# A decoder of six layers on one core: the small work of PEER, BiDAF and MoE placed differently

## The reference

```python
x = x + causal_attention(layernorm(x))
x = x + cross_attention(layernorm(x), ctx)
x = x + peer(layernorm(x))            # product-key experts
x = x + band_attention(layernorm(x))
x = x + bidaf(layernorm(x), ctx)
x = x + moe(layernorm(x))             # 8 experts, the top 2
```

## Time and profile before

| what | value |
|---|---|
| median of three runs | 3894.4 us |
| the profiled execution | 3891.91 us, its span 3889.9 us |
| busy, share of the span | PE 86%, DVE 71%, POOL 51%, ACT 30% |
| PEER | 913 to 2535 us |
| BiDAF | 2980 to 3262 us |
| MoE's head | 3262 to 3356 us |
| MoE's tiles | 3361 to 3890 us |

### The profile page before, as it was taken

The page is one execution under the profiler, slowest core; times in us unless marked ns, Lnnn a source line. Parts: engine busy times, 40 slices in busy tenths (PEclk is TensorE's granted clock), DMA queues, the critical chain, the costliest instruction groups (busy, mean ns, idle before and its releaser), DMA issues. The chain is left out here.

```text
span 3889.9 us, 93119 instructions
## 1 busy us (share of the span) xinstructions
PE 3336.4 (86%) x33694; PEld 2822.4 (73%) x33695; DVE 2759.0 (71%) x10928; ACT 1156.3 (30%) x2660; POOL 1993.4 (51%) x2200
## 2 busy tenths in 40 slices
PE   6999957875798998989999989878887888599998
PEld 4777735554688888888888888845564667599998
DVE  6666634556999999999999999768885443533333
ACT  1344435442222222222222222146663111122221
POOL 4444335540766666666666666768882000133332
PEclk8999969987899999999999999989997886699999
DMA  5444334442000000000000000045441002566665
GB/s 152 106 113 107 97 91 120 119 110 100 2 2 2 2 2 2 2 2 2 2 2 2 2 2 2 2 126 128 127 125 40 24 24 100 152 184 178 187 177 139
DMA packets 256102, 277.73 MB, mean 71 GB/s; under 512 B 44002, under 2 KB 200674, under 8 KB 255202
## 3 DMA queue, kind: packets, MB, share of 16 engines
q1 hardware_dynamic: 242081, 253.69, 22.8%
q0 software_dynamic: 13632, 18.91, 3.2%
HBM read 187.63 MB, written 72.29 MB: 67 GB/s over the span
## 5 line engine op out<-in xcount | busy, mean ns | idle before, releaser
L1163 POOL TENSOR_TENSOR peer_hot_v<-peer_hot_e,peer_parts 80x512 bf16<-80x512 bf16 x768 | 1045.0, 1386 | 456.4 <-DVE peer_hot_e L1202 443.2
L1008 PE MATMUL peer_ps_u<-peer_up,peer_g 128*128 128x256 f32 x2048 | 544.8, 414 | 0.6 <-DVE x_all L1319 0.6
L989 PEld LDWEIGHTS peer_ps_h<-peer_xnT,peer_down 128*128 128x128 f32 x4096 | 507.0, 195 | 17.0 <-DMA peer_down<-in_peer_down 2.5
L989 PE MATMUL peer_ps_h<-peer_xnT,peer_down 128*128 128x128 f32 x4096 | 506.9, 278 | 2.2 <-DMA peer_down<-in_peer_down 2.2
L999 PE MATMUL peer_ps_w<-peer_hot_v,peer_hot_u 80*128 80x32 bf16 x12288 | 347.7, 177 | 173.1 <-DVE peer_g L1214 111.7
L999 PEld LDWEIGHTS peer_ps_w<-peer_hot_v,peer_hot_u 80*128 80x128 bf16 x12288 | 336.5, 97 | 197.0 <-DVE peer_hot_u L1206 123.0
L1008 PEld LDWEIGHTS peer_ps_u<-peer_up,peer_g 128*128 128x128 f32 x2048 | 402.1, 206 | 56.7 <-issue 1.0
L1086 ACT ACTIVATE peer_g<-peer_ps_h 128x512 f32<-128x512 f32 x256 | 152.8, 597 | 904.8 <-PE peer_ps_h L989 904.7
L1206 DVE TENSOR_TENSOR peer_hot_u<-peer_count,peer_uvT 80x2048 bf16<-80x2048 bf16 x256 | 344.8, 1347 | 0.0
L2058 POOL DMA_INDIRECT moe_xg<-moe_xn_rows,moe_source x71 | 70.4, 991 | 420.7 <-DVE moe_target L2165 389.6
L2064 POOL DMA_INDIRECT out<-moe_y,moe_target x71 | 113.0, 1592 | 311.9 <-DVE moe_y L2195 308.9
(11 more groups left out here) (362 smaller groups left out, 6974.1 us busy)
## 6 DMA issues: line engine op xcount, KB each, us to landing
moe_w<-in_moe_w SPq DMA_DIRECT2D x142, 512.0 KB
causal_qs<-causal_qscratch SPq DMA_DIRECT2D x32, 384.0 KB, 3.9
cross_qs<-cross_qscratch SPq DMA_DIRECT2D x32, 384.0 KB, 3.7
band_qs<-band_qscratch SPq DMA_DIRECT2D x32, 384.0 KB, 4.0
moe_w<-in_moe_w SPq DMA_DIRECT2D x8, 1024.0 KB, 11.8
causal_qscratch<-causal_part SPq DMA_DIRECT2D x32, 192.0 KB, 2.6
causal_kscratch<-causal_part SPq DMA_DIRECT2D x32, 192.0 KB, 2.0
causal_ks<-causal_kscratch SPq DMA_DIRECT2D x32, 192.0 KB, 4.2
```

The source lines that it names most:

```text
L989: mm = nc.tensor.matmul(ps_h[:, n % 2, k * P:(k + 1) * P], down[:, c, 4 * n + k, :], xnT[:, par, c, :], start=(c == 0), stop=(c == DC - 1))
L1008: mm = nc.tensor.matmul(ps_u[:], g[:, par, v, :], up[:, v, :], start=(v == 0), stop=(v == EV - 1))
L1163: ins = nc.gpsimd.tensor_tensor(hot_v[0:SEL, n % RING, part], hot_e[0:SEL, n % RING], w, ALU.mult)
```

## The change

- PEER: `norm` and `candidates` go from DVE to POOL, at the start of `macro` ahead of the hots. The Exp becomes eight with `accum_out`, which also makes `es`, and the reduction on DVE goes.
- BiDAF: `halves` takes the place of `each`, fully written out. In each half-step h every part works on batch h minus its own lag. `project` is split in three; norm of c is on POOL. For MoE, each batch gets its own moments, roots (an integer guess and three Newton steps on DVE), normalised rows (POOL), store, transposes, logits and top choices, with lags of 2 to 4. The constants of MoE are made at half-step 3, and `w2` is loaded 1 MB at a time in half-steps 2 to 9. The tensors and semaphores for this are in a new `Route`, which is closed at the end of the kernel.
- MoE's head keeps what follows the top choices. One-hots are f16, in four groups of 8 tiles with 3 DVE instructions each; the name of a token is one f16 number, so 71 columns take the place of 142. `expert` is made after the first group, and SP's loads of w1 wait for it alone.

```diff
-                nc.scalar.activation(ew[:], ew[:], ACT.Exp).then_inc(exp_out, 1)
+                for h in range(NQ):
+                    ins = nc.scalar.activation(ew[:, h, :], ew[:, h, :], ACT.Exp, accum_out=es[:, h, :])
+                ins.then_inc(exp_out, 1)
...
+            def norm(t):
+                wait(pool, xt_done, t)
+                nc.gpsimd.tensor_scalar(xn[:], x_all[:, t, :], mean[:, t, :], rstd[:, t, :], ALU.subtract,
+                                        ALU.mult).then_inc(xn_ready, 1)
+
+            def candidates(t):
+                pool.wait_ge(halves_done, t + 1)
+                wait(pool, code_ready, t)
...
+                pool.wait_ge(roots_ready, 1)
+                norm(0)
+                norm(1)
+                candidates(0)
...
             def macro(t, par):
+                if there(t + 2):
+                    norm(t + 2)
+                if there(t + 1):
+                    candidates(t + 1)
...
-                steps.link(nc.vector.tensor_reduce(es[:], ew[:], AX.X, ALU.add))
...
+        def halves(steps):
+            for h in range(B + 5):
+                for part, back in steps:
+                    b = h - back
+                    if 0 <= b < B:
+                        part(streams[b % NS], b // NS, b)
...
+            for h in range(B + 4):
+                if h < B:
+                    fetch(streams[h % NS], h // NS, h)
+                if h == 1:
+                    weights()
+                if 0 <= h - 2 < B:
+                    store(streams[h % NS], (h - 2) // NS, h - 2)
+                if 0 <= h - 3 < B:
+                    store_rows(streams[(h - 3) % NS], (h - 3) // NS, h - 3)
+                if 2 <= h < 2 + E:
+                    sp.dma_start(route.w2[:, h - 2], w2_in[:, h - 2]).then_inc(route.weights, 16)
...
+                wait(pe, z.l_used, n - 1)
...
+            def project_a(z, n, b):
                 pe.wait_ge(z.a_used, n + 1)
+                for t in range(TT):
+                    tile = z.p3[:, t * D:(t + 1) * D]
+                    for c in range(DC):
+                        nc.tensor.matmul(tile, z.aT[:, c, t * P:(t + 1) * P], wl[:, DC + c, :], start=(t == 0 and c == 0), stop=False)
...
+            def turn_x(z, n, b):
+                pe.wait_ge(z.xn_ready, n + 1)
+                pe.wait_ge(z.acol_ready, min(n + 2, B // NS))
+                for t in range(TT):
+                    for c in range(DC):
+                        at = (t * DC + c) * P
+                        mm = nc.tensor.transpose(z.p1[:, at:at + P], route.xn[:, z.k, t, c * P:(c + 1) * P], ident[:])
+                mm.then_inc(z.xt_done, 1)
+
+            def logits(z, n, b):
+                pe.wait_ge(z.xt_used, n + 1)
+                pe.wait_ge(route.loaded, 16 * route.NLOAD)
+                for t in range(TT):
+                    for c in range(DC):
+                        mm = nc.tensor.matmul(z.p1[:, t * E:(t + 1) * E], route.xnT[:, t, c, :], route.wr[:, c, :],
+                                              start=(c == 0), stop=(c == DC - 1))
+                mm.then_inc(z.l_done, 1)
+
+            halves([(turn_prob, 1), (col, 1), (turn, 0), (attend, 1), (q2c, 1), (row, 0), (project_a, 1), (scores, 0),
+                    (project_ca, 1), (turn_x, 3), (top, 0), (project_c, 1), (logits, 3)])
...
+            def take_x(z, n, b):
+                act.wait_ge(z.xt_done, n + 1)
+                if b > 0:
+                    act.wait_ge(streams[(b - 1) % NS].l_done, (b - 1) // NS + 1)
+                nc.scalar.activation(route.xnT[:].rearrange("p t c q -> p (t c q)"), z.p1[:], ACT.Copy).then_inc(z.xt_used, 1)
+
+            halves([(take_prob, 1), (take, 0), (take_a, 1), (exps, 0), (eexp, 0), (take_x, 3)])
+
+        @block.gpsimd
+        def _(pool):
+
+            def norm(z, n, b):
+                if b == 0:
+                    pool.wait_ge(ready, 1)
+                wait(pool, z.q2c_done, n)
+                for t in range(TT):
+                    ins = nc.gpsimd.tensor_scalar(z.c[:, t, :], x_all[:, b * TT + t, :], mean[:, b * TT + t, :],
+                                                  rstd[:, b * TT + t, :], ALU.subtract, ALU.mult)
+                ins.then_inc(z.c_ready, 1)
+
+            def norm_rows(z, n, b):
+                pool.wait_ge(z.roots_ready, n + 1)
+                wait(pool, z.xt_done, n)
+                wait(pool, route.rows_out[z.k], 16 * n)
+                for t in range(TT):
+                    ins = nc.gpsimd.tensor_scalar(route.xn[:, z.k, t, :], x_all[:, b * TT + t, :], stats.mv[:, b * TT + t, 0:1],
+                                                  route.guess[:, z.k, t:t + 1], ALU.subtract, ALU.mult)
+                ins.then_inc(z.xn_ready, 1)
+
+            norm(streams[0], 0, 0)
+            halves([(norm, -1), (norm_rows, 3)])
...
+            def roots(z, n, b):
+                links = Steps(dve, root_step)
+                tiles = slice(b * TT, (b + 1) * TT)
+                var, g, i, q = route.var[:, z.k], route.guess[:, z.k], route.half[:, z.k], route.sq[:, z.k]
+                wait(dve, z.xn_ready, n)
+                for t in range(TT):
+                    ins = nc.vector.bn_aggr(stats.mv[:, b * TT + t, :], stats.moments[:, b * TT + t, :])
+                links.link(ins)
+                links.link(nc.vector.tensor_scalar(var, stats.mv[:, tiles, 1], EPS, None, ALU.add))
+                links.link(nc.vector.tensor_scalar(i, var.bitcast(I32), 1, None, ALU.logical_shift_right))
+                links.link(nc.vector.tensor_scalar(g.bitcast(I32), i, -1.0, float(0x5f3759df), ALU.mult, ALU.add))
+                for k in range(3):
+                    links.link(nc.vector.tensor_tensor(q, g, g, ALU.mult))
+                    links.link(nc.vector.tensor_tensor(q, q, var, ALU.mult))
+                    links.link(nc.vector.tensor_scalar(q, q, -0.5, 1.5, ALU.mult, ALU.add))
+                    ins = nc.vector.tensor_tensor(g, g, q, ALU.mult)
+                    if k < 2:
+                        links.link(ins)
+                ins.then_inc(z.roots_ready, 1)
+                links.again()
+
+            def take_logit(z, n, b):
+                tiles = slice(b * TT, (b + 1) * TT)
+                dve.wait_ge(z.l_done, n + 1)
+                nc.vector.tensor_tensor(route.logit[:, tiles, :], z.p1[:, 0:TT * E].rearrange("p (t e) -> p t e", e=E),
+                                        route.br[:].unsqueeze(1).broadcast_to((P, TT, E)), ALU.add).then_inc(z.l_used, 1)
+
+            def pick(z, n, b):
+                dve.wait_ge(z.l_used, n + 1)
+                for t in range(b * TT, (b + 1) * TT):
+                    ins = nc.vector.max(route.top[:, t, :], route.logit[:, t, :])
+                steps.link(ins)
+                for t in range(b * TT, (b + 1) * TT):
+                    nc.vector.max_index(route.topi[:, t, :], route.top[:, t, :], route.logit[:, t, :])
+
...
+            halves([(take_logit, 4), (take_col, 1), (make_m, 0), (add, 2), (make_row, 0), (make_wad, 1), (product, 1),
+                    (moments, 2), (rowmax, 0), (normalise, 0), (find_top, 0), (batch_row, 0), (roots, 2), (pick, 4), (constants, 3)])
...
-            sp.wait_ge(table_ready, 1)
+            sp.wait_ge(expert_ready, 1)
...
-                for h in range(HOTS):
-                    mm = nc.tensor.matmul(ps_y[:, 0, 0:2 * JT], rowhot[:, n % 2, h, :],
-                                          tilehot[:, n % 2, h, :, :].rearrange("p a j -> p (a j)"),
-                                          start=(n == 0 and h == 0), stop=(n == NHOT - 1 and h == HOTS - 1))
-                mm.then_inc(hot_used, 1)
+                for t in range(n * FEW, (n + 1) * FEW):
+                    for k in range(TOPE):
+                        mm = nc.tensor.matmul(ps_y[:, 0, 0:JT], rowhot[:, t, :, k], tilename[:, t, :, k],
+                                              start=(t == 0 and k == 0), stop=(t == TILES - 1 and k == TOPE - 1))
+            mm.then_inc(hot_used, 1)
...
+            def one_hot(out, values, n, few):
+                steps.link(nc.vector.tensor_tensor(out[:, few], iota2[:, 0:n, :].unsqueeze(1).broadcast_to((P, FEW, n, TOPE)),
+                                                   values[:, few, :].unsqueeze(2).broadcast_to((P, FEW, n, TOPE)), ALU.is_equal))
+
             for n in range(NHOT):
-                wait(dve, hot_used, n - 1)
-                few = slice(n * HOTS // TOPE, (n + 1) * HOTS // TOPE)
-                nc.vector.tensor_tensor(rowhot[:, n % 2], iota16[:].unsqueeze(1).broadcast_to((P, HOTS, P)),
-                                        rowb[:, few, :].rearrange("p t k -> p (t k)").unsqueeze(2).broadcast_to((P, HOTS, P)),
-                                        ALU.is_equal)
-                for h in range(HOTS):
-                    t, k = divmod(HOTS * n + h, TOPE)
-                    ins = nc.vector.scalar_tensor_tensor(tilehot[:, n % 2, h], iota16[:, 0:JT].unsqueeze(1).broadcast_to((P, 2, JT)),
```

(32 more changed lines are left out.)

## The result

The changed kernel takes 3812.3 us (median of 4 runs, 3807.8 to 3816.4) against 3896.7 us (3894.1 to 3904.4) of the kernel before in 4 runs: a ratio of 0.978, 95% interval 0.9761 to 0.9798. The forecast was 3782 with a range of 3742 to 3828, so sign and range hold, and the gain is 84 us where 112 were forecast.

| stage | before | after | difference | forecast |
|---|---|---|---|---|
| PEER | 1622.1 | 1585.3 | -36.7 | -45 |
| all after PEER up to BiDAF | 445.9 | 446.6 | +0.7 | 0 |
| BiDAF | 280.7 | 309.6 | +28.9 | 0 (-20 to +30) |
| MoE's head to the first gather | 94.7 | 25.5 | -69.2 | -68 |
| what follows | 533.6 | 531.5 | -2.1 | +1 |

A forecast was written before the change was run, and what follows sets the result against it. VectorE's stream was taken to bound PEER, an engine-to-engine chain BiDAF, and serial work MoE's head. PEER -45, BiDAF 0, head -68 and end +1 gave -112 on 3891.9: 3780, 3782 as median, range 3742 to 3828 us.

The forecast's parts named there:

- the head: MoE's head up to the first gather: 94.7 us shrinks to 26.6, so -68 us, bounds -58 and -70.
- the mechanism in PEER: PEER: DVE's stream sets the tile's period; three pieces leaving it save 1.50 us per tile, -45 us in all.
- so I keep the loss as it is: PEER: DVE's hots keep losing the present 57 us, 1.8 per tile, to collisions with POOL's work.
- Rival 2: PEER: POOL's pieces hold up DVE, or PE is next; PEER worth 0 to -20, 3807 to 3827 us; chance 0.15.
- The price of candidates(0): PEER's opening: DVE waits for POOL's first candidates, 1.7 us against 0.91 on DVE; with the norms before it +1.5 us.
- The cycle: BiDAF: one chain from take_logit through PE, DVE and ACT sets the half-step, 9.4 + 5.5 = 14.9 us at full clock.
- I take 0.88: BiDAF: PE's granted clock taken as 0.88, so 9.4/0.88 + 5.5 plus 0.2 makes a half-step of 16.4 us.
- the prediction's own sign of being wrong: BiDAF: turns over 17.5 us apart would show the forecast wrong; 16.4 us apart would show it right.
- the four norms: BiDAF: POOL's four norms against DVE's tensor_scalars were to add 0.2 us to each half-step.
- The ends: BiDAF: first four half-steps 53 us, the first of them 8.5; behind the sixteenth 21 us and a barrier of 1.1.
- the head's rival price: MoE's head: if one-hots compare at rowhot's present rate, each of four groups takes 2.1 us more, +8.6 us.
- Rival 3: BiDAF: the cycle is longer, 17.5 to 18.5 us; BiDAF +15 to +30, 3797 to 3812 us; chance 0.14.

The follow-up runs named there:

- experiment 4: The changed kernel with norm, candidates or the sum of es put back on VectorE, one at a time: 3828.9, 3826.4 and 3815.6 us.
- pe_filled: The changed kernel with 16 more transposes of ident per half-step on PE, where it waits ahead of turn in BiDAF: 3794.7 us, ratio 0.9746.
- experiment 6: The changed kernel with BiDAF's norm of c on VectorE, between moments and rowmax, norm_rows still on POOL: 3813.2 us, ratio 0.9783.
- experiments 2 and 3: Changed kernel with take_logit earlier, PE's wait filled or two Newton steps: 3807.1, 3794.7, 3794.7 us; roots in DVE's gap, then also ctx loaded earlier: 3786.2, 3775.9 us.
- roots_in_gap: The changed kernel with roots moved between moments and rowmax on VectorE, where it waits for the scores: 3786.2 us, ratio 0.9729.

## Why the prediction was right, and where it was off

**Right: the head.** -69.2 against -68, each term as worked out: rowhot 1.22 us for 1.2, the two of 128x1136 at 0.74 for 0.742, the cast to the first one-hot 10.7 us with ew for 10.8, the first gather 25.5 us after MoE's first instruction for 26.6. The one-hots compare at the f16 rate of the earlier trace rows and not at that of rowhot before.

**Right: the mechanism in PEER, 8 us too much.** A tile takes 47.5 us for 47.3. The missing 8 are waits and collisions that I costed at nothing: the hots 3.4 us longer in all (482.1 for 478.7), 2.1 in which DVE waits for candidates, 1.9 more for ACT's `peer_wT` (3.1 for 1.2) and 0.7 more for PE (8.1 for 7.4), 8.1 together; the last two are no more than this stage moves from kernel to kernel. The step "so I keep the loss as it is" holds for the total, but by two shifts against each other: experiment 4 has the candidates add 13.5 us of collisions and norm's leaving DVE remove 7.9. Rival 2 therefore holds for one piece in small, and so does its sign: DVE does wait for cand_ready, twice, 3.9 us in all with the opening. The price of candidates(0) was right (1.7, took 1.62); inside a tile the five additions take 2.8 us (4.0 once) and norm 1.22, and POOL had room for both. ACT's eight Exps (0.20 + 0.19 us each) made no wait, as costed.

**Mis-sized: BiDAF's clock.** The cycle is as predicted: turn waits for take_logit (25.3 us in all), behind roots of 3.16 us; from top's end to the next turn are 5.55 us (3112.04 to 3117.59), forecast 5.5. At full clock PE's part, from turn to top, is 9.72 us (3156.31 to 3166.03 in pe_filled), forecast 9.4, and the half-step 15.2, forecast 14.9. What failed is the sentence "I take 0.88". The whole stage before had 0.82, which would have given 17.2 us, and 0.88 was chosen above it between two windows. The mean was 0.83 from 3010 to 3175, so 9.72/0.83 = 11.7 us; and the cycle's own part was slower than the mean, 18.1 - 5.5 = 12.6 us, as 0.77 would make it. I took the clock for a mean that is the same for all of PE's work. But PE's one long wait of a half-step is the 2.04 us ahead of turn, and the low stretch begins there: it falls on turn, attend, q2c and project_a, which are in the cycle, and has ended when project_c and logits run, which aren't. 10.7 + 5.5 + 0.2 = 16.4 became 12.6 + 5.5 = 18.1, and the prediction's own sign of being wrong, turns over 17.5 us apart, was there. The windows of three whole half-steps say that the clock is all that was added to 15.2 us: 16.9 us at 0.90, 18.5 at 0.80 and 19.8 at 0.76 (the two halves together) have lost 1.7, 3.7 and 4.7 us to it, and what remains is 15.2, 14.8 and 15.1. Of the four norms for which 0.2 stood, experiment 6 took two off POOL and the half-step stayed.

Two runs show it from both sides. Filling PE's wait with idle work gives a clock of 0.94 (1.00 once ctx is no longer late) and 16 us back; taking 0.8 us out of the wait gives these 0.8 us per half-step and leaves the clock at 0.84. The Trainium skill ("TensorE: Matmul & The Clock Gate", A second HAM failure mode) describes a kernel in which PE idles briefly and often between groups of matmuls and the clock goes up and down, at a loss of throughput. The trace agrees: a wait of 2.04 us ahead of eleven turns and of 2.83 ahead of one, and windows between 0.69 and 0.93.

**The ends** were 8.6 us too short (+0.8, +3.0 and +4.8), the last of them at a clock of 0.69 from 3209 to 3254, with one batch left to fill PE. The 0.8 is POOL's norm ahead of the first turn (experiment 6 has that turn 1.0 us earlier); the rest I put down to the clock, which no run shows apart. Why the clock stays low for longer in one half-step than in the next, with the same wait ahead of both, these runs don't settle. Two things weren't tried: the one-hots alone, and w2's loads back in the head. The load of w2 cost the changed kernel no wait of a turn, as forecast; in the shorter half-steps of experiments 2 and 3 it did. In the head's rival price, 4 x 2.1 is 8.4 and not 8.6, and nothing hangs on it.

**Rival 3** (17.5 to 18.5 us per half-step, 3797 to 3812) is what came to pass in the half-step, and the time is at its upper end. It was held at 0.14, and the row that spoke for it was the 0.75 of the earlier trace rows; I let the better window outweigh it although the change puts PE's wait in one place.

## What to carry to other kernels

Where a cycle runs through several engines, look for what stands last in the period of an engine that others wait for: 15 small dependent instructions (3.2 us) at the end of VectorE's list cost 34 us over 16 batches more than in the gap in which VectorE waited anyhow, where PE still waits 0.7 us for them in most half-steps. Don't divide by a mean clock: ask on whose matmuls the low stretch falls, which is those behind PE's longest wait; if that wait can't go, PE can be given work to do in it. A piece moved to POOL is worth its length on DVE less what it stretches there: here 10 of 28 us for the candidates, but 15 for norm, whose length is 10, so each piece wants a run of its own. And moving an instruction out of one collision can put another into it, so look at every group of the engine and not only at the one that was to get shorter.

## What the runs showed of the hardware

- Behind a wait of 2.04 us, in a half-step in which it waited for nothing else as long, PE ran at 1.2 GHz for most of 10 us (0.53 from 3117.6 to 3127.6); with 16 useless transposes in place of the wait two windows stood at 1.00.
- On POOL a 128x256 f32 tensor_scalar with two operands per partition takes 1.22 us (0.40 on DVE), and the candidates' five additions 1.62 us undisturbed and 2.8 beside DVE's hots (0.87 on DVE).
- The mean of hot_e on DVE was 488 ns with candidates on DVE, 522 with candidates and norm on POOL, and 552 with candidates alone on POOL, with hot_v beside it in each case.
- A 120 KB load issued right behind a 1 MB one on the same queue lands after 5.6 us, ahead of it after 2.4. In pe_filled seven turns waited 1.2 to 2.1 us for it, in roots_in_gap five 0.4 to 1.5; in the changed kernel none.
- A comparison of 128x2240 on DVE took 1.37 us on average and 2.07 once its place was beside POOL's hot_v.
